# A graph layer on one core: the idle rows of the expert table are filled from ScalarE's queue, and a chunk's local numbers are asked for apart from its penalties

## The reference, cut to what matters

```
xn = layernorm(x)
el, er = (xn @ W_src + b_src) . attn_l, (xn @ W_dst + b_dst) . attn_r      # per head
e   = leaky_relu(el[src] + er[dst])
a   = exp(e - segment_max(e, dst)) / segment_sum(exp(...), dst)
gnn = segment_sum((xn @ W_val + b_val)[src] * a, dst)
mix = linear_attention(xn @ W_qkv, elu features) @ W_out + b_out
x   = x + gnn + mix
x   = x + moe(layernorm(x))        # softmax router, top 2 of 8, gelu experts of width 256
```

## Time and profile before

| what | us |
|---|---|
| median of three executions | 2637.53 |
| the profiled execution, its own time | 2638.22 |
| its span in the trace | 2636.4 |
| PE busy, share of the span | 2248.7 (85%) |
| DVE busy | 1685.3 (64%) |
| POOL busy | 1265.3 (48%) |
| ACT busy | 1048.8 (40%) |
| first matmul of the projection begins | 85.27 |
| first chunk's `both_ends` on DVE | 603.48 |
| first and last store of a closed tile issued | 769.6, 1843.4 |

### The profile page before, as it was taken

The page is one execution under the profiler, slowest core; times in us unless marked ns, Lnnn a source line. Parts: engine busy times, 40 slices in busy tenths (PEclk is TensorE's granted clock), DMA queues, the critical chain, the costliest instruction groups (busy, mean ns, idle before and its releaser), DMA issues. The chain is left out here.

```text
span 2636.4 us, 49572 instructions
## 1 busy us (share of the span) xinstructions
PE 2248.7 (85%) x11641; PEld 1672.0 (63%) x11665; DVE 1685.3 (64%) x3935; ACT 1048.8 (40%) x2822; POOL 1265.3 (48%) x1431
## 2 busy tenths in 40 slices
PE   5699999977996398999898898988778775998998
PEld 4577777754664265666666666666456555887887
DVE  4544444437996298998878888887466662443444
ACT  1111111115653165565555555554445432332333
POOL 0000000027775276776666677770146464554554
PEclk9899999987998699999989999999788777999999
DMA  4122222247776276777677777771978544665665
GB/s 152 35 70 70 70 62 69 70 126 224 226 222 177 79 214 193 217 217 196 191 196 205 203 205 214 208 216 53 342 199 210 153 135 128 219 218 170 212 215 180
DMA packets 200299, 445.44 MB, mean 169 GB/s; under 512 B 46086, under 2 KB 72070, under 8 KB 200044
## 3 DMA queue, kind: packets, MB, share of 16 engines
q0 software_dynamic: 94784, 309.82, 40.7%
q1 hardware_dynamic: 95124, 124.23, 15.4%
q10 hardware_dynamic: 10136, 8.39, 1.0%
HBM read 352.33 MB, written 94.70 MB: 170 GB/s over the span
## 5 line engine op out<-in xcount | busy, mean ns | idle before, releaser
L633 POOL DMA_INDIRECT arena<-v_table,idx x832 | 817.6, 983 | 383.7 <-issue 207.6
L1677 PE MATMUL ps<-arena 128*128 128x260 f32 x3328 | 913.8, 413 | 12.4 <-DVE ps L1223 12.0
L1677 PEld LDWEIGHTS ps<-arena 128*128 128x128 f32 x3328 | 608.6, 198 | 143.4 <-issue 55.2
L782 ACT ACTIVATE arena<-ps x832 | 502.7, 604 | 299.4 <-issue 185.0
L1226 DVE TENSOR_TENSOR arena<-arena,ps 128x512 f32<-128x512 f32 x832 | 555.5, 669 | 0.0
L1510 PE MATMUL ps<-ident,arena 128*128 128x128 f32 x1170 | 198.8, 283 | 63.9 <-DMA arena<-tab,e_idx 34.7
L605 POOL TENSOR_SCALAR ag<-ag 128x1 f32<-128x1 f32 x49 | 10.8, 221 | 487.1 <-DVE ag L1032 487.0
L1505 PE MATMUL ps<-arena 128*128 128x24 bf16 (+4 forms) x1602 | 233.6, 271 | 6.8 <-DVE key_cols L1120 3.0
L1477 DVE TENSOR_TENSOR xt_lo<-ps,xt_hi 128x512 fp32r<-128x512 f32 x112 | 77.5, 692 | 243.1 <-ACT xt_hi L875 243.1
L1139 DVE TENSOR_SCALAR arena<-ps,p_no 128x512 bf16<-128x512 f32 x208 | 154.9, 745 | 118.8 <-PE ps L1505 118.4
L773 ACT ACTIVATE arena<-arena 128x24 bf16 x832 | 179.6, 216 | 101.2 <-issue 91.4
(11 more groups left out here) (276 smaller groups left out, 3816.3 us busy)
## 6 DMA issues: line engine op xcount, KB each, us to landing
arena<-in_x SPq DMA_DIRECT2D x98, 256.0 KB, 2.9
tab<-arena SPq DMA_DIRECT2D x98, 256.0 KB, 4.9
arena<-v_table,idx POOLq DMA_INDIRECT x832
v_table<-arena SPq DMA_DIRECT2D x49, 260.0 KB, 2.9
agg<-arena SPq DMA_DIRECT2D x49, 260.0 KB
arena<-agg SPq DMA_DIRECT2D x49, 260.0 KB, 4.2
q_table<-arena SPq DMA_DIRECT2D x49, 128.0 KB, 2.8
dq<-q_table SPq DMA_DIRECT2D x49, 128.0 KB, 4.1
```

The lines of the kernel that those rows point to most:

```text
L633: pool.indirect_dma_start(vg[:, v * U + i, :], None, v_table, bass.IndirectOffsetOnAxis(ap=idx[:, j, i:i + 1], axis=0))\
L782: act.activation(halves(fin[:, bass.ds(room, DH)], HALF), halves(ps[:, bass.ds(room, 2 * D)], D)[:, :, 0:HALF], ACT.Copy).then_inc(s("act_ ...
L1677: return pe.matmul(sums[h], hot[:, i // V, i % V, :], vg[:, b * U + i, h * HALF:(h + 1) * HALF], start=False, stop=(i == U - 1), skip_grou ...
```

## The change

The two fills move from SP's program to ACT's, behind ACT's wait for its weights and ahead of `wv_hi`, and get a semaphore of their own. `chunk_in` is split: the penalties (`ends_asked`) stay behind `weights` in step 10, with their own semaphores `pen_in0` and `pen_in1`, for which DVE now waits in `max_up`. The local numbers (`locals_asked`) move to step 2 of the next chunk's loop turn for the chunk three ahead, behind a wait for PE's use of the buffer (`lc_mm`), that is eight steps ahead of the penalties of the same chunk.

```
@@ SP
             sp.wait_ge(s("tables_in"), 32)
-            for k in range(TOP):
-                sp.dma_start(tab[NO_ROW:TAB_ROWS, k * D:(k + 1) * D], x[NP - 1:NP, :].broadcast_to([TAB_ROWS - NO_ROW, D]))\
-                    .then_inc(s("tok_cleared"), 16)
             for d in range(NT):
                 tile_store(d)
@@ POOL, ahead of the tokens
-            pool.wait_ge(*past("tok_cleared", 64))
+            pool.wait_ge(*past("tok_cleared", 32))
+            pool.wait_ge(s("tab_filled"), 32)
@@ ACT, setup
             act.wait_ge(s("weights_in"), WEIGHT_DMAS * 16)
+            for k in range(TOP):
+                act.dma_start(tab[NO_ROW:TAB_ROWS, k * D:(k + 1) * D], x[NP - 1:NP, :].broadcast_to([TAB_ROWS - NO_ROW, D]))\
+                    .then_inc(s("tab_filled"), 16)
             act.activation(wv_hi[:], wv, ACT.Copy).then_inc(s("pw_hi"), 1)
@@ ACT, edges
-            def chunk_in(c, b):
+            def locals_asked(c, b):
                 act.dma_start(locals_[:, b, :], local_table[bass.ds(c * U, U), :].rearrange("s e -> (s e)").unsqueeze(0))\
                     .then_inc(s(f"chunk_in{b}"), 16)
+
+            def ends_asked(c, b):
                 act.dma_start(pen[:, b, :], pen_table[bass.ds(c * U, U), :].unsqueeze(1).broadcast_to([U, H, P + 1]))\
-                    .then_inc(s(f"chunk_in{b}"), 16)
+                    .then_inc(s(f"pen_in{b}"), 16)
...
                     elif i == 10:
                         weights(c + 1, (k + 1) % RING)
                         if ahead:
-                            chunk_in(c + 3, b)
+                            ends_asked(c + 3, b)
+                    elif i == 2 and ahead:
+                        act.wait_ge(s("lc_mm"), c * V + 2 * V)
+                        locals_asked(c + 3, b)
@@ DVE
-            def max_up(c, b):
+            def max_up(c, b, r):
                 dve.wait_ge(s("ev_tp"), c + 1)
+                dve.wait_ge(s(f"pen_in{b}"), 16 * (r + 1))
@@ PE
-                    pe.wait_ge(s(f"chunk_in{b}"), 32 * (r + 1))
+                    pe.wait_ge(s(f"chunk_in{b}"), 16 * (r + 1))
```

More of the change, by code:

```diff
@@ L68 @@
 SEMAPHORES = (
-    "acc_shut", "bk_mm", "blr_set", "bo_split", "chunk_in0", "chunk_in1", "dlt", "dst_out",
+    "acc_shut", "bk_mm", "blr_set", "bo_split", "chunk_in0", "chunk_in1", "pen_in0", "pen_in1", "dlt", "dst_out",
     "dummy_set", "e_gelu", "e_hhi", "e_hmm", "e_ht", "e_htp", "e_lin", "e_out", "e_sub", "e_tp", "e_xhi",
@@ L81 @@
     "tables_in", "tabs_ready", "tabs_ready2", "tile_sum", "tok_put", "v_set", "w_hi", "w_lo", "weights_in",
-    "wo_in", "xn_st0", "xn_st1", "xn_st2", "xn_st3")
+    "tab_filled", "wo_in", "xn_st0", "xn_st1", "xn_st2", "xn_st3")
 def quarter(j, n=NT, u=4):
@@ L106 @@
     **chained("setup_in", 16 * SETUP_DMAS, ("fin_st", 16 * NT)),
-    **chained("tables_in", 32, ("tok_cleared", 64)),
+    **chained("tables_in", 32, ("tok_cleared", 32)),
     **chained("p_row", 3, ("tok_zero", 4)),
@@ L806, in chunk @@
                         if ahead:
-                            chunk_in(c + 3, b)
+                            ends_asked(c + 3, b)
+                    elif i == 2 and ahead:
+                        act.wait_ge(s("lc_mm"), c * V + 2 * V)
+                        locals_asked(c + 3, b)
             act.wait_ge(s("tables_in"), 32)
             act.wait_ge(s("g_out"), 2)
-            chunk_in(0, 0)
-            chunk_in(1, 1)
+            for c in range(2):
+                locals_asked(c, c)
+                ends_asked(c, c)
             act.wait_ge(s("er_split"), 5)
@@ L819, in _ @@
             weights(0, 0)
-            chunk_in(2, 0)
+            act.wait_ge(s("lc_mm"), V)
+            locals_asked(2, 0)
+            ends_asked(2, 0)
             chunks(act, chunk)
@@ L1264, in chunk @@
                     elif i == 4:
-                        max_up(c + 1, b)
+                        max_up(c + 1, b, lap_round(n, k + 1, 2))
                     elif i == 5:
@@ L1293, in _ @@
             leaked(0)
-            max_up(0, 0)
+            max_up(0, 0, 0)
             max_down(0, 0)
```

## The result

The changed kernel takes 2619.48 us, the median of six executions (2611.68 to 2626.31); before took 2636.64 beside it (2632.41 to 2639.71). The ratio is 0.9932, 95% interval 0.9909 to 0.9955. A second set of executions of the changed kernel gave 2612.13 against 2628.75, 0.9924 (0.9902 to 0.9945). It is faster by some 0.7%; the forecast of 2640 us and its range from 2624 both miss it.

The account below looks back on a forecast made before the run. The prediction saw a setup chain and, in the edge stage, PE waiting for a store held behind thin one-engine fills. From 2638.22 us, + 78 - 66 - 6 - 4 = + 2 gave 2640 us, range 2624 to 2658.

Parts of the forecast that it names:

- The hold of ACT: Setup: ACT held 82.8 to 92.2 us in issuing the second fill, 86 taken; the setup costs 78 us (73 to 89).
- The sorting: Setup, PE sorting edge tables after idling: three more slow microseconds of its clock cost 1.4 us, at most 6.
- Rivals 3 and 4: Setup: 3, ACT isn't held, 2562 us, 6%; 4, ACT is held for both fills, 2732 us, 3%.
- The hole: Edge stage, chunk 11 to 12: PE's wait for the first closed tile's store goes, 66 us won.
- Fill traffic and local numbers: Edge stage: fill traffic gone and local numbers asked sooner end PE's waits for `pen_table`; 6 us won, bounds 0 and 10.5.
- The limit: Edge stage: POOL finishes issuing chunk 11 at 819.12, DVE wants it at 829.62, so at most 10.5 us gained.
- rival 1: Edge stage paced by POOL's gathers, so the small terms give nothing: 2650 us, 25%.
- Closings: Tile closings in the edge stage: ACT goes on 0.63 us sooner; 11 us won or 6 lost, 4 won taken.
- Rival 2: Edge stage: the small terms pay in full, 10 and 11 us, giving 2629 us; 17%.
- The bound given for being wrong: Edge stage, first `both_ends` to last store: forecast wrong if it shortens by less than 64 or more than 90 us.

Follow-up runs that it names:

- e1: Against the kernel before, only the two fills moved to ACT's queue; local numbers and penalties still asked together in step 10: 2645.24 us, 1.0037.
- e4: Against the kernel before, fills stay on SP and both loads in step 10; only the semaphores of local numbers and penalties are apart: 2637.96 us, 1.0022.
- f2: Against the kernel before, fills stay on SP, local numbers asked in step 2 and penalties in step 1 of the next chunk: 2596.71 us, 0.9862.

## Why the prediction was wrong

- **The hold of ACT: right.** 84.76 us for 82.8 to 92.2; ACT's copy at 120.49 for 121.5; the first tile 75.8 us late for 78. The sorting took 0.4 us longer (11.63 us for 11.24), where 1.4 were allowed for the clock. Rivals 3 and 4 fell with it.
- **The hole: right.** 66.4 for 66. The two terms as measured give 75.8 - 66.4 = + 9.4; e1, which has them and a part of the next, came out 7 to 12 us slower than before.
- **Fill traffic and local numbers: right in size, not in its reason, and wrong in its limit.** Chunks 0 to 11 gained 5.8 us for 6. The reason given was that PE's waits for penalties go. In e1 they do go there, from 14.6 us to 0.2, and it gains 2.0; in e4 the fills' traffic stays, the waits are only set apart, and it gains 7.4. How the two act together isn't shown. The limit, that "the stage cannot get more than 10.5 us ahead", came from POOL's lead in one chunk; chunks 24 to 51 alone got 18.5 ahead. POOL's lead isn't fixed. In chunks 0 to 11 of the changed kernel POOL does set the pace: they take 220.35 / 11 = 20.0 us each, and it waits 6.7 us for PE to free its ring. In chunks 24 to 51 it waited 84.4 us for PE in before and still 67.5 in the changed kernel, so it follows when PE gets faster. There rival 1 falls.
- **Closings: the step that failed.** "I take 4 won." Chunks 24 to 51 gave 18.5 us in one profile and 24.1 in the other. The prediction counted PE's waits alone, and those came out near its upper end: 57.4 to 47.9 is 9.5 us, for 11. It took off 6 for the issue moved to step 2, which cost nothing that the runs show, and let only a part of the rest count, because DVE waits for PE. And it left out the clock: behind the long waits PE runs at 1.2 GHz for some microseconds (the windows of e4 above), and 10.0 of the 18.5 us are the same matmuls done in less time (562.8 to 552.8 us busy; in the second profile 17.0 of 24.1). The clock was worked out for the setup, from the earlier trace rows, and not asked about in the stage with 48 waits. That PE's waits in f2 are 39.7 us bears out the 39.4 that the prediction worked out for an ACT in step.
- The net, + 2 forecast, came out at about - 17 to - 20 by medians and ratios. Rival 2 (2629), given 17%, had the late closings paying in full, but not the clock, and lies 9.5 us above what was measured. The bound given for being wrong was met: the edge stage from first `both_ends` to last store shortened by 1239.9 - 1149.2 = 90.8 us.

What stays open: why the projection up to the first chunk takes 3.7 us less, how much of e1's longer chunks (630.5 against 625.2) is more than variation, and why the clock falls more often in one execution than in another at the same waits.

## What to carry to other kernels

When an engine that others wait for gets late, price its lateness in two terms, the wait and the matmuls that run at half clock behind it; here the second was at least as large as the first, though it varies far more, and one DMA issue in a bad place cost 0.6 us in each of chunks 24 to 51, where most tiles close. Put issues where the engine has room, not behind the last thing that a chunk's end waits for. And before moving a long transfer to another queue, look at its row count: one row fewer in the main piece made it several times shorter, and the question of whose queue it holds nearly went away.

## What the runs showed of the hardware

- The issue of a fill of 1153 rows (DMA share 0.07) returned after 1.2 us (31.38 to 32.59); the next issue on the same queue was held 84.76 us, and as long at another place of the setup (84.65). While SP's queue was held in before, ACT's issues were not: none took more than 0.495 us.
- Cut into 1152 rows and one, the fills ran at 118 GB/s instead of 26 (DMA share 0.67), and all four issues returned in 15.07 us.
- On ACT, copies standing ahead of a DMA issue ran beside it: two of together 0.49 us cost the next snapshot nothing (1.22 us against 1.21 without them), while a second issue of 0.46 us cost 0.66.
- A wait of 1.82 us of PE was followed by some 3 us at the 1.2 GHz level (1529.7 to 1533.1 in e4). Longer waits were followed by such a fall more often than shorter ones, but not each time.
